# Taking six groups of products of a constant tile out of a two-layer kernel

## The reference

```
x = x + L0_attn(L0_cond_GRU(cond, x))      # recurrence over 32 steps, then attention, 16 heads of 128
x = x + L0_ffn(causal_conv(x) + b)         # silu(gate) * up, rms norm, down; quantised weights and rows
x = x + L1_attn(L1_cond(x, cond))          # modulated attention, 16 heads of 16; then rotary attention, 16 heads of 128
x = x + L1_ffn(causal_conv(x))             # relu(x w_fc)^2 w_proj, with w dequantised from 5 bits
```

```
h = jax.nn.silu(bit_linear(x, w_gate)) * bit_linear(x, w_up)
h = rms_norm(h, ln_weight)
return bit_linear(h, w_down)
```

## Time and profile before

| what | us |
| --- | --- |
| median of 3 runs | 1330.69 |
| lowest, highest run | 1329.5, 1332.3 |
| the profiled execution | 1327.77 |
| its span, from the first to the last instruction | 1325.9 |
| TensorE busy in the span | 1281.7 (97%) |
| VectorE busy | 1129.5 (85%) |
| ScalarE busy | 809.4 (61%) |

### The profile page before, as it was taken

The page is one execution under the profiler, slowest core; times in us unless marked ns, Lnnn a source line. Parts: engine busy times, 40 slices in busy tenths (PEclk is TensorE's granted clock), DMA queues, the critical chain, the costliest instruction groups (busy, mean ns, idle before and its releaser), DMA issues.

```text
span 1325.9 us, 25724 instructions
## 1 busy us (share of the span) xinstructions
PE 1281.7 (97%) x9778; PEld 943.8 (71%) x9778; DVE 1129.5 (85%) x2921; ACT 809.4 (61%) x1592; POOL 85.1 (6%) x88
## 2 busy tenths in 40 slices
PE   5999999999999999999999889999999999999998
PEld 2444444688878888888887676667777878787867
DVE  4899999889989889898979798588888888879885
ACT  4999999874656565656555864644545554545323
POOL 0000000101020101011011000000000000000000
PEclk9999999999999999999999999999999999999999
DMA  9433343521202020202030320100000000000000
GB/s 378 141 72 80 80 104 87 171 79 49 63 11 80 2 81 1 81 1 81 11 123 27 149 63 11 41 1 17 1 25 1 25 2 23 9 9 9 9 1 24
DMA packets 26536, 73.69 MB, mean 56 GB/s; under 512 B 3992, under 2 KB 5156, under 8 KB 25136
## 3 DMA queue, kind: packets, MB, share of 16 engines
q1 hardware_dynamic: 25840, 71.10, 17.2%
q10 hardware_dynamic: 576, 0.98, 0.2%
HBM read 49.26 MB, written 22.81 MB: 54 GB/s over the span
## 4 chain that ended last, share of the span: by engine, by line
PE 57%; DVE 31%; ACT 8%; issue 3%; DMA 1%; SPq 0%; DVEq 0%; ACTq 0%
DVE work L1920 10%; PE psum L990 7%; PE psum L1021 6%; PE psum L599 6%; PE psum L766 4%; PE psum L1035 4%; PE psum L1063 4%; PE psum L646 3%; PE psum L570 2%; PE psum L579 2%; PE psum L1002 2%; PE psum L936 2%; DVE h_all L1920 2%; PE psum L698 1%; PE psum L1015 1%
## 5 line engine op out<-in xcount | busy, mean ns | idle before, releaser
L646 PE MATMUL psum<-h_all,w_big 128*128 128x256 f32 x1024 | 235.2, 382 | 1.3 <-ACT work L1353 1.2
L646 PEld LDWEIGHTS psum<-h_all,w_big 128*128 128x128 f32 x1024 | 190.0, 190 | 32.5 <-issue 5.7
L1920 DVE SCALAR_TENSOR_TENSOR work<-work,taps 128x240 f32<-128x240 f32 (+28 forms) x518 | 139.9, 344 | 0.0
L599 PE MATMUL psum<-w_big,h_all 128*64 128x512 f32 x512 | 121.1, 595 | 0.0
L990 PE MATMUL psum<-work,w_big 128*128 128x256 f32 x512 | 118.1, 379 | 0.5 <-DVE gru_mem L2533 0.5
L766 PE MATMUL psum<-w_big,gru_mem 128*128 128x256 f32 x512 | 113.7, 379 | 0.5 <-ACT gru_mem L1399 0.5
L1021 PE MATMUL psum<-w_big 128*128 128x256 f32 x448 | 105.4, 384 | 2.6 <-ACT w_big L1660 2.6
L766 PEld LDWEIGHTS psum<-w_big,gru_mem 128*128 128x128 f32 x512 | 96.9, 190 | 14.9 <-ACT gru_mem L1399 0.6
L990 PEld LDWEIGHTS psum<-work,w_big 128*128 128x128 f32 x512 | 96.0, 190 | 13.5 <-DVE gru_mem L2533 0.9
L1021 PEld LDWEIGHTS psum<-w_big 128*128 128x128 f32 x448 | 82.9, 190 | 22.0 <-issue 6.7
L2531 DVE TENSOR_TENSOR gru_mem<-psum,trig 128x256 f32<-128x256 f32 x128 | 53.7, 420 | 41.1 <-PE psum L990 37.0
(11 more groups left out here) (360 smaller groups left out, 2561.0 us busy)
## 6 DMA issues: line engine op xcount, KB each, us to landing
value_rows<-w_emb SPq DMA_DIRECT2D x128, 128.0 KB, 2.3
work<-value_rows SPq DMA_DIRECT2D x16, 1024.0 KB, 5.8
w_big<-in_Wq SPq DMA_DIRECT2D x2, 2048.0 KB, 16.8
w_big<-in_Wo SPq DMA_DIRECT2D x2, 2048.0 KB, 21.7
out<-w_big SPq DMA_DIRECT2D x15, 256.0 KB, 2.1
x_res<-out SPq DMA_DIRECT2D x15, 256.0 KB, 2.8
w_big<-in_Wv SPq DMA_DIRECT2D x1, 2048.0 KB, 18.0
w_big<-in_Wk SPq DMA_DIRECT2D x1, 2048.0 KB, 24.6
```

What stands on the lines that cost most here:

```text
L599: mm = pe.matmul(bank(4 + n)[j * B:(j + 1) * B, :], h_all[:, k, :, 2 * pair + j], w_big[:, 2, k * H * HD + n * 512:k * H * HD + (n + 1) * ...
L646: mm = pe.matmul(bank(n % 2)[:, o * TA:(o + 1) * TA], w_big[:, s, k * H * HD + at:k * H * HD + at + HD], h_all[:, k, bass.ds(i * BA, BA), ...
L1920: ins = dve.scalar_tensor_tensor(dst[:, :, lag:], src[:, :, :T - lag], tap, dst[:, :, lag:], ALU.mult, ALU.add)
```

## The change

The five direct calls of `keep_clock` and the argument 14 of `gate_up(e, 1, 14)` are taken out. The helper and its `idle` arguments stay in the file and are called with 0. All waits, all other instructions and their order stay.

```diff
                 gate_up(c, 3)
-                keep_clock(16, 0)
                 cond_scores(0, 1)
-                keep_clock(4, 0)
                 down_turn(c, 0)
...
                 if begun:
-                    keep_clock(8, 6)
                     turn_y(e)
...
-                    gate_up(e, 1, 14)
+                    gate_up(e, 1)
...
                     down(e, 0)
-                    keep_clock(24, 0)
                     rot_outputs(i, 0)
...
                     elif rot:
-                        if second:
-                            keep_clock(14, 6)
                         rot_project(i, 0, range(0, 8))
```

## The result

The changed kernel took 1334.03 us in the median, the kernel before beside it 1330.11. The ratio is 1.0037, with an interval of 1.0027 to 1.0047, so the change costs 3.6 to 6.3 us, 4.9 in the middle. (Every ratio here is an estimate over all executions and comes close to that of the means; it is not the quotient of the two medians, which would be 1.0029.) The change is slower by more than the 0.2% that can be told apart, inside the stated range and on the side of the forecast, but 0.22 points of a per cent more than forecast: 4.9 us where the forecast had 2.0.

The account below looks back on a forecast made before the run. TensorE, 97% busy, was not taken to set the end where the products run: the chain of waits passes through other engines. Direct terms 0 plus one clock fall of 2.0 us on 1330.69 gave 1332.7 us, range 1329.0 to 1338.0.

Parts of the forecast that it names:

- Direct terms 0: At all six places, removing 8.7 us of TensorE products gains 0 directly, between a loss of 0 and a gain of 0.3.
- Place 2: 4 products before `down_turn(c, 0)`: in the way by about 0.3 us, taken in by a later 1.49 us wait; 0.
- One fall, behind place 5: 24 products before `rot_outputs`: 3.8 us idle makes TensorE's clock fall once, costing 2.0 us (0.9 to 3.8); chance 0.40.
- The high end: Behind `rot_outputs`' emptied place: both L1015 groups and L960 all run at half rate, costing 3.8 us.
- Places 1, 3, 4 and 6 stay within that.: Idle stretches at these four places lie within the 2.40 us that did no harm, so no loss there.
- place 6: 14 products before `rot_project`: direct 0, 2.0 us idle; a fall there priced 0.5, between 0 and 1.3.
- The rival with several falls: Clock falls at several places, or stays down from place 4 to place 5: 5.2 us slower, 1336 us; chance 0.23.
- place 3: 8 products before `turn_y`: direct 0, 2.1 us idle; a fall there costs 1.3 us, with nothing to take it up.
- place 4: 14 products between the gate and up products: direct 0, 2.3 us idle; a fall leaves some 0.5 of 1.3 us.
- place 1: 16 products before `cond_scores(0, 1)`: direct 0, about 1.7 us idle; a fall leaves 0 after the 1.49 us wait.
- The first rival: TensorE's clock holds at every emptied place, so no loss: 1330.7 us; chance 0.33.
- The rival "faster": Place 2's 0.3 us on the path, or a neighbour the products slowed: 1330.4 us by the rows; over 0.2% faster, chance 0.04.

Follow-up runs that it names:

- no5: Only the 24 products before `rot_outputs` taken out of the kernel before, the other 56 kept: 1333.14 us, ratio 1.0020.
- no12: Only the 20 products before `cond_scores(0, 1)` and `down_turn(c, 0)` taken out of the kernel before: 1330.30 us, ratio 1.0006.
- keep5: Of the kernel before's products only the 24 before `rot_outputs` stay, the other five places are emptied: ratio 1.0017, 2.3 us.
- step1: Kernel before plus 14 products of 512 columns before the state is transposed in step 1 of the recurrence: 1329.13 us, ratio 0.9988.

## Why the prediction was right, and where not

- **Direct terms 0.** Right. All idle stretches have the forecast lengths and the old releasers, and by the clock of the executions nothing is left over within a microsecond. 8.7 us of work went and none of it was gained. Place 2 went as said: L722 starts 1.25 us after the scores (769.12 against 767.87) where it took 1.45, and the wait behind, before L968, grew from 1.49 to 1.69 us and took the 0.2 us in.
- **One fall, behind place 5.** Half right. It falls there in both profiles without these products, and the low clock of all eleven executions of `no5` says that it is the rule. The first group takes 2.09 instead of 1.14 us, as said; the second does not get longer than 2.07 (1.84 and 1.71). The price forecast was 2.0 (0.9 to 3.8). Place 5 alone measured 2.7 by time, but 1.1 and 0.8 in the two profiles, so it is open whether the price was sized well. The high end was read wrongly: the 2.07 us of the second group are not all work, since the first group, of as many products, takes 1.14. At half rate the three groups take 2 x (1.14 + 1.07 + 1.14) = 6.7 us, 2.1 more than the 4.57 of before and not 3.8. But it was not the only fall.
- **"Places 1, 3, 4 and 6 stay within that."** This is the step that failed, and with it the total: 2.0 us forecast, 4.9 measured, to which the prediction's own chances gave 0.36 ("slower") against 0.60 for no change that can be told. The bound from below, 2.40 us of idle time without a fall, came from one execution. The repeated kernel before has the same 2.40 us and falls behind it. One row that shows no fall is no proof that none comes; the set 3, 4, 6 costs 2.0 us and place 6 alone 1.6, and the clock fell near the end behind 1.70 us.
- **The rival with several falls** (0.23 in the prediction) is what happened. It was priced at +5.2 and measured +4.9; that its inner split (1.3 for place 3, 0.5 for place 4, 0.5 for place 6, 0 for place 1) agrees in sum is luck, since place 3 alone measured 0.1 us and place 6 alone 1.6. Behind places 1 and 2 the changed kernel's profile shows 3.2 us where I had 0: the wait of 1.49 us before L970 does take up the delay ahead of it, but the fall came behind that wait, at L916, `down` and `cond_project`, which are on the chain (the 20 L916 take 3.84 us there, and in the kernel before 2.40). Whether the empty places 1 and 2 cause that fall stays open: `no12` can't be told from no change, and neither its profile nor that of `keep5` has the fall.
- **The first rival** (the clock holds, 0.33) is out: no execution of the changed kernel had a clock over 0.994.
- **The rival "faster" (0.04)** had the right sign nowhere.

## What to carry to other kernels

An instruction that computes nothing, put where an engine idles anyway and over before the wait ends, costs nothing there, and on TensorE it can hold the clock; one that outlasts the wait delays what stands behind it, by some 0.6 us in `step1`. The time lost or gained goes with the clock, so judge such a group by the mean granted clock over many executions, not by the one in the profile. Where idle stretches of 1.7 us or more remain, look at what runs right behind them on the chain, since that is what ran at half rate here. And look for what the cure itself does: 14 wide products in the second step of the recurrence gained 1.6 us, these and 24 more ahead of the first inputs lost 4.8, and 70 narrow ones lost 6.3.

## What the runs showed that I had not expected

The same idle stretch of 1.7 to 2.4 us let the clock fall in one profile and not in another. In the kernel before, the executions with a clock of 1.000 took 1327.0 us and those with 0.996 took 1331.8. And TensorE stood still for 1.9 to 3.1 us inside an unbroken row of small products in the kernels with 38 and 70 products more, each time until 1.3 to 1.6 us after a packet of instructions had landed.
